# A graph network kernel's start and end: where the scale search, the last power, the ring writes and the last row sums stand

## What is computed

```python
# layer 0
h = max(layernorm(x), 0)
mask = adj > 0
e[b,j,k,:] = relu(h[b,j] @ W1a + (h[b,j] - h[b,k]) @ W1b + b1)   # H = 192
hm[b,j,:] = sum over k of e[b,j,k,:] * mask[b,j,k]
x = x + hm @ W2 + deg * b2                                        # deg = row sums of mask
# layer 1
h = max(layernorm(x), 0)
x = x + (adj @ h) @ W.T
```

## Time and profile before

| | us |
|---|---|
| runs, median (lowest to highest, 3 runs) | 842.24 (841.91 to 843.48) |
| the profiled execution, in all | 845.98 |
| its span, first to last instruction | 844.1 |
| PE busy in the span | 810.6 (96%) |
| DVE busy | 809.9 (96%) |
| ACT busy | 794.9 (94%) |
| POOL busy | 611.5 (72%) |
| mean granted clock of PE | 0.98 |

### The profile page before, as it was taken

The page is one execution under the profiler, slowest core; times in us unless marked ns, Lnnn a source line. Parts: engine busy times, 40 slices in busy tenths (PEclk is TensorE's granted clock), DMA queues, the critical chain, the costliest instruction groups (busy, mean ns, idle before and its releaser), DMA issues.

```text
span 844.1 us, 26648 instructions
## 1 busy us (share of the span) xinstructions
PE 810.6 (96%) x8242; PEld 715.0 (85%) x8243; DVE 809.9 (96%) x2894; ACT 794.9 (94%) x2246; POOL 611.5 (72%) x1174
## 2 busy tenths in 40 slices
PE   4879999999999999999999999999999999999996
PEld 2447888898889888988998899888988898889884
DVE  6969999999999999999999999999999999999993
ACT  4969999999999999999999999999999999999992
POOL 1966777777777777777777777777777777777762
PEclk8979999999999999999999999999999999999996
DMA  9800000000000000000000000000000000000000
GB/s 337 327 1 2 7 9 21 21 21 15 21 20 21 9 21 21 20 15 21 21 21 9 20 21 21 15 21 20 21 9 21 21 20 14 21 21 21 15 3 21
DMA packets 26705, 27.55 MB, mean 33 GB/s; under 512 B 3520, under 2 KB 24512, under 8 KB 25536
## 3 DMA queue, kind: packets, MB, share of 16 engines
q1 hardware_dynamic: 25488, 25.37, 8.9%
q10 hardware_dynamic: 1072, 0.43, 0.2%
HBM read 21.59 MB, written 4.19 MB: 31 GB/s over the span
## 4 chain that ended last, share of the span: by engine, by line
PE 90%; DVE 4%; issue 2%; ACT 2%; DMA 1%; SPq 0%; ACTq 0%; DVEq 0%
PE ring L414 48%; PE ring L442 8%; PE prep L471 5%; PE post L514 4%; PE post L501 3%; PE post L508 3%; PE post L502 3%; PE prep L479 3%; PE prep L482 2%; PE prep L477 2%; DVE acc L826 2%; PE post L506 2%; DMA x_all<-x_nbf_dram 1%; PE prep L473 1%; DVE onehot_space L812 1%
## 5 line engine op out<-in xcount | busy, mean ns | idle before, releaser
L826 DVE SCALAR_TENSOR_TENSOR acc<-ring,acc 128x384 f32<-128x384 f32 x896 | 488.6, 545 | 0.6
L572 ACT COPY ring<-P 128x384 f32<-128x384 f32 x1024 | 466.6, 509 | 19.3 <-DVE acc L826 11.4
L414 PE MATMUL ring<-PQ,onehot_space 128*128 128x192 f16 x4096 | 417.0, 247 | 4.5 <-ACT ring L572 2.2
L414 PEld LDWEIGHTS ring<-PQ,onehot_space 128*128 128x128 f16 x4096 | 328.0, 99 | 39.4 <-issue 13.5
L922 POOL TENSOR_SCALAR start<-P,spare 128x192 f32<-128x192 f32 x128 | 128.4, 1003 | 134.8 <-ACT P L622 133.8
L946 POOL TENSOR_TENSOR row_space<-row_space 128x192 f32<-128x192 f32 x256 | 153.4, 599 | 25.3 <-ACT row_space L610 8.2
L812 DVE TENSOR_SCALAR onehot_space<-mask_all 128x512 f16<-128x512 f16 x512 | 158.1, 311 | 0.0
L442 PE MATMUL ring<-PQ,owner 128*128 128x384 f16 (+1 forms) x512 | 93.9, 306 | 0.0
L414 PE MATMUL ring<-PQ,onehot_row 128*128 128x192 f16 x768 | 84.3, 246 | 0.5 <-DVE onehot_row L874 0.3
L610 ACT ACTIVATE row_space<-ring 128x576 f32<-128x576 f32 x128 | 83.3, 651 | 0.7 <-PE ring L414 0.7
L826 DVE SCALAR_TENSOR_TENSOR acc<-ring,start 128x384 f32<-128x384 f32 x128 | 71.1, 556 | 5.3 <-PE ring L414 1.3
(11 more groups left out here) (138 smaller groups left out, 1431.9 us busy)
## 6 DMA issues: line engine op xcount, KB each, us to landing
onehot_space<-adj_kbj_dram SPq DMA_DIRECT2D x8, 1024.0 KB, 17.3
adj_again<-adj_kbj_dram SPq DMA_DIRECT2D x128, 64.0 KB, 2.0
x_all<-x_nbf_dram SPq DMA_DIRECT2D x8, 512.0 KB, 19.0
out_dram<-x_all SPq DMA_DIRECT2D x32, 128.0 KB, 1.9
consts<-consts_dram SPq DMA_DIRECT2D x1, 192.0 KB, 2.4
scratch<-w1a_dram ACTq DMA_DIRECT2D x2, 48.0 KB, 4.2
scratch<-w1b_dram ACTq DMA_DIRECT2D x2, 48.0 KB, 6.7
scratch<-b_dram ACTq DMA_DIRECT2D x1, 96.0 KB, 10.1
```

What stands on the lines that cost most here:

```text
L414: last = nc.tensor.matmul(to, hot(s), parts[:, part, H:2 * H], start=False, stop=(part == 1), skip_group_check=True)
L572: return nc.scalar.copy(slots[to][:, bank_], src.unsqueeze(1).broadcast_to([N, PER_BANK, H]))
L826: return nc.vector.scalar_tensor_tensor(sums, slots[to][:, bank_], 0.0, start[:, :, :] if first else sums, ALU.max, ALU.subtract if first ...
```

## The change

- **PE**: codes(1) to codes(3) run whole, then L398; codes(4), then L402; the loop has parts 5 and 6 only. In every step the wait for the row sums stands between L501 and L502 instead of ahead of L501. After the codes, ring banks 0 to 3 are written before the tables, with a `ring_ready` of their own.
- **DVE**: `largest()` stands behind mask 2, `largest_of_rows()` behind mask 4, `scale()` behind mask 5, `second_parts()` behind mask 6. The four one-hots of chunk 0 come ahead of the wait for the last copies, two of chunk 1 ahead of the tables. In step 128 DVE adds the last graph's rows, which POOL did.
- **ACT**: L654 stands behind codes(4) and the two lead steps; parts 1 to 3 are a loop, part 4 is written out, 5 to 7 a loop. The steps begin when `any_loops` and the first `ring_ready` are there; chunk 2 of graph 0 waits for the second. In the tail both h2 of a pair are made together, those of the last pair behind the sums' copy of step 132.
- **POOL**: norm1(3) stands right behind norm1(2), ahead of the `spare` chain; `load_any` comes after the first `start`.
- **SP**: the last four graphs are stored two by two.

Unchanged lines are cut except next to a change, and indentation is reduced by eight.

```diff
--- before.py
+++ after.py
@@ -369,16 +369,17 @@
             adj(b + BODY + 1)
-    sp.wait_ge(y_ready, B // 2)
-    sp.dma_start(out[:, B - STORE:B, :], x_all[:, B - STORE:B, :]).then_inc(stored, 16)
-    sp.wait_ge(stored, 16 * B // STORE)
+    for done in range(B - STORE + 2, B + 1, 2):
+        sp.wait_ge(y_ready, done // 2)
+        sp.dma_start(out[:, done - 2:done, :], x_all[:, done - 2:done, :]).then_inc(stored, 16)
+    sp.wait_ge(stored, 16 * (B // STORE - 1 + STORE // 2))
...
 def _(pe):
-    def codes(g, quads=range(QUADS)):
+    def codes(g):
         pe.wait_ge(mask_ready, g + 1)
-        for q in quads:
+        for q in range(QUADS):
             quad = g * QUADS + q
@@ -392,15 +393,17 @@
     codes(0)
-    codes(1, range(QUADS // 2))
+    codes(1)
+    codes(2)
+    codes(3)
...
                      stop=True).then_inc(largest_seen, 1)
-    codes(1, range(QUADS // 2, QUADS))
+    codes(EARLY)
     pe.wait_ge(largest_ready, 2)
     nc.tensor.matmul(post[:, N:N + 1], ones_row[:, :], to_scale[0:1, 1:2], start=True, stop=True).then_inc(largest_seen, 1)
-    with pe.Fori(2, LATE) as g:
+    with pe.Fori(EARLY + 1, LATE) as g:
         codes(g)
@@ -494,11 +497,11 @@
                     pe.wait_ge(summed, b * REGULAR)
-                    pe.wait_ge(hm_row_ready, b)
                     if not main:
...
                         nc.tensor.matmul(head_ps, acc_space[:, (u - 1) // 2 % 2, s, heads[(u - 1) % 2]], ident, start=(s == 0), stop=False, is_transpose=True)
+                    pe.wait_ge(hm_row_ready, b)
                     last = nc.tensor.matmul(head_ps, row_heads[(u - 1) % 2], ownerT[:, (u - 1) % QUAD, :], start=False, stop=True)
@@ -526,18 +529,17 @@
 
-    pe.wait_ge(rows_counted, 1)
-    nc.tensor.matmul(tables[:, 0, :], ones[:, :], rows, start=True, stop=True)
-    nc.tensor.matmul(tables[:, 1, :], rows, ones[:, :], start=True, stop=True).then_inc(rows_summed, 1)
...
     pe.wait_ge(code_kj_ready, B // QUAD)
-    pe.wait_ge(code_jk_ready, B // QUAD)
-    write_ring(range(QUADS))
+    write_ring(range(QUADS)).then_inc(ring_ready, 1)
+
+    pe.wait_ge(rows_counted, 1)
+    nc.tensor.matmul(tables[:, 0, :], ones[:, :], rows, start=True, stop=True)
+    nc.tensor.matmul(tables[:, 1, :], rows, ones[:, :], start=True, stop=True).then_inc(rows_summed, 1)
@@ -571,6 +573,17 @@
 
+    def second_norm(b, u, t):
+
+        wait_apart(act, norm2_ready, pairs(b, u, t, -5 if u % 2 else -6))
+        if exists(b - 9):
+            act.wait_ge(transposed, transposes(b - 2 if u % 2 else b - 3))
+        k = (u - 5) // 2 % 2
+        for g in range(2) if not exists(b - 1) else ((u - 5) % 2,):
+            of = b - 5 - (u - 5) % 2 + g
+            nc.scalar.activation(h2[:, k, 2 * g, :], x_all[:, of, :], ACT.Relu, bias=shift2[:, k, g:g + 1],
+                                 scale=rstd2[:, k, g:g + 1]).then_inc(h2_ready, 1)
@@ -578,6 +591,8 @@
                     act.wait_ge(p_ready, b + 1)
+                if i == 2 and isinstance(b, int) and b == 0:
+                    act.wait_ge(ring_ready, 2)
                 if i == 2 and exists(b - 1):
@@ -597,6 +612,8 @@
                 nc.scalar.copy(sums_T[:, parts, :], sums_T_ps[:, parts, :]).then_inc(even_T_ready, 1)
+            if i == 0 and isinstance(b, int) and b == B + 4:
+                second_norm(b - 1, u - 1, t)
             if i == 0 and u % 2 and exists(b - 2):
@@ -620,14 +637,8 @@
                 nc.scalar.copy(P[:, (u + 1) % 2, :], pq_ps[:, 0:H]).then_inc(p_ready, 1)
-            if i == 4 and exists(b - 5):
-
-                wait_apart(act, norm2_ready, pairs(b, u, t, -5 if u % 2 else -6))
-                if exists(b - 9):
-                    act.wait_ge(transposed, transposes(b - 2 if u % 2 else b - 3))
-                k, g = (u - 5) // 2 % 2, (u - 5) % 2
-                nc.scalar.activation(h2[:, k, 2 * g, :], x_all[:, b - 5, :], ACT.Relu, bias=shift2[:, k, g:g + 1],
-                                     scale=rstd2[:, k, g:g + 1]).then_inc(h2_ready, 1)
+            if i == 4 and exists(b - 5) and (u % 2 or exists(b - 1)) and not (isinstance(b, int) and b == B + 3):
+                second_norm(b, u, t)
             if i == 4 and exists(b + 3):
@@ -648,19 +659,18 @@
     codes(0)
-    codes(1)
-    codes(2)
+    with nc.scalar.Fori(1, EARLY) as g:
+        codes(g)
+    codes(EARLY)
+    act.wait_ge(norm1_ready, 1)
+    lead(step, hi=-1)
     act.wait_ge(scale_ready, 1)
...
                          scale=to_scale[:, 2:3]).then_inc(first_parts_ready, 1)
-    codes(3)
-    act.wait_ge(norm1_ready, 1)
-    lead(step, hi=-1)
-    with nc.scalar.Fori(EARLY, PARTS) as g:
+    with nc.scalar.Fori(EARLY + 1, PARTS) as g:
         codes(g)
...
     some = load_any(nc.scalar)
-    act.wait_ge(tables_ready, 1)
     act.wait_ge(ring_ready, 1)
@@ -752,30 +762,43 @@
 
+    def hot(b, u, i, s):
+
+        return nc.vector.tensor_scalar(onehot[:, hot_of(u), i, s, :, :], code_kj[:, bass.ds(b, QUAD), :],
+                                       2.0 * (SLOTS * i + s) + 1.0, None, ALU.is_equal)
+
+    def first_hot():
+
+        for s in range(SLOTS):
+            last = hot(0, 0, 0, s)
+        last.then_inc(onehot_ready, 1)
...
     norm1_stats(1)
+    mask(2)
     largest()
-    mask(2)
-    largest_of_rows()
     moments(0)
     norm1_stats(2)
-    scale()
     mask(3)
     norm1_stats(3)
+    mask(4)
+    largest_of_rows()
     moments(1)
-    mask(4)
-    second_parts()
     mask(5)
+    scale()
     norm1_stats(4)
     mask(6)
+    second_parts()
     norm1_stats(5)
...
     moments(3)
+    dve.wait_ge(code_kj_ready, 1)
+    first_hot()
@@ -787,9 +810,8 @@
 
-    dve.wait_ge(p_ready, 1)
-    second_part(0, 0)
-
+    hot(0, 0, 1, 0)
+    hot(0, 0, 1, 1)
     dve.wait_ge(rows_summed, 1)
@@ -800,23 +822,21 @@
     nc.vector.tensor_scalar(loops[0:1, 1, :], fits[0:1, :], -float(LOOPED), float(LOOPED), ALU.mult, ALU.add)
+    nc.vector.tensor_copy(row_count[:, :], owned)
+    dve.wait_ge(p_ready, 1)
+    second_part(0, 0)
     dve.wait_ge(owned_sums, 1)
     nc.vector.tensor_scalar(loops[0:1, 0, :], tables[0:1, 3, :], float(LOOPED), None, ALU.mult)
-    nc.vector.tensor_copy(row_count[:, :], owned)
     chain(nc.vector.tensor_tensor(first_row[:, :], tables[:, 2, :], owned, ALU.subtract))
...
 
-    def hot(b, u, i, s):
-
-        return nc.vector.tensor_scalar(onehot[:, hot_of(u), i, s, :, :], code_kj[:, bass.ds(b, QUAD), :],
-                                       2.0 * (SLOTS * i + s) + 1.0, None, ALU.is_equal)
...
         i = u % QUAD
-        if exists(b - i + QUAD):
-            last = hot(b - i + QUAD, u - i + QUAD, i, s)
+        of = b - i + QUAD
+        if exists(of) and not (isinstance(of, int) and of == 0 and i == 1 and s < 2):
+            last = hot(of, u - i + QUAD, i, s)
             if s == SLOTS - 1:
@@ -829,6 +849,13 @@
         at = bass.ds(b + 1, 1)
+        if not main and b == B:
+
+            dve.wait_ge(relu_row_ready, B)
+            sums = relu_rows[(u - 1) % 2][:, 0, :]
+            nc.vector.tensor_tensor(sums, sums, relu_rows[(u - 1) % 2][:, 1, :], ALU.add).then_inc(half_row_ready, 1)
+            dve.wait_ge(half_row_ready, B)
+            nc.vector.tensor_tensor(sums, sums, relu_rows[(u - 1) % 2][:, 2, :], ALU.add).then_inc(hm_row_ready, 1)
         for i in range(CHUNKS):
@@ -908,9 +935,6 @@
 
-    for s in range(SLOTS):
-        last = hot(0, 0, 0, s)
-    last.then_inc(onehot_ready, 1)
     lead(step)
@@ -937,7 +961,7 @@
             nc.gpsimd.tensor_tensor(x_all[:, of, :], x_all[:, of, :], bias[:, :, :], ALU.add).then_inc(xb_ready, 1)
-        if exists(b - 1):
+        if exists(b - 1) and exists(b):
@@ -1009,6 +1033,7 @@
     norm1(2)
+    norm1(GROUPS - 1)
@@ -1019,12 +1044,10 @@
     pool.wait_ge(spare_step, 3)
-    some = load_any(nc.gpsimd)
-    pool.wait_ge(tables_ready, 1)
     pool.wait_ge(p_ready, 1)
...
     lead(step, lo=-1)
-    norm1(GROUPS - 1)
+    some = load_any(nc.gpsimd)
     graphs(nc.gpsimd, step, some)
```

## The result

The changed kernel takes 844.63 us (median of 20 runs, lowest 843.18), the kernel before on the same chip 842.7 (20 runs): ratio 1.0026, 95% interval 1.0019 to 1.0034. In a second comparison the ratio was 1.0029 (1.0017 to 1.0042). One of the 20 runs took 1020.49 at a mean granted clock of 0.75, and the ratio leaves it out. The prediction was 838.8 with 841.4 as its upper end: wrong in sign and outside its range.

The account below looks back on a forecast made before the run. PE and DVE were taken to bound the middle, its length unchanged. Front 2.3, end 1.0 and last store 0.1 summed to 3.4, taken from the median 842.24: 838.8 us, range 836.8 to 841.4.

Parts of the forecast that it names:

- the sentence on the middle: Middle steps, PE busy 99.69 and DVE 99.53 of 100 us: the change gains only by an earlier start and shorter end.
- Slower: PE's clock: Rival, first steps: over 10 us more at PE's lower clock make the change slower; with 12 us 844.8; chance 0.05.
- The opening: 2.3 predicted: Up to graph 0's first accumulation: POOL's chain ends last, so L826 comes at 54.6 instead of 56.92, 2.3 us gained.
- Quad 8 at 18.85: ACT's copies in the opening: quad 8 is copied at 18.85 instead of 20.51, 1.66 us earlier.
- I take 0.7 of the waits as covered: ACT's loop entry: 0.7 of 2.7 us of operations and waits is hidden, bounds 0 and 1.3; L593 comes at 44.5.
- DVE's stalls of 0.45 and 1.4: DVE in the opening: it stands 0.45 us ahead of L709 and 1.4 ahead of scale(), with no loss to ACT.
- L1003 at 34.8: POOL's chain in the opening: L1003 moves from 32.61 to 34.8, and norm1(2)'s power follows at 39.75.
- After the copies: Tables and one-hots before graph 0: tables 0.7 us later, one-hots 1.6 less, net 0.9 earlier; owner's product at 53.7.
- 56.92: Time of the first L826 in the profiled execution of the kernel before; the front gain was taken from it.
- The copies don't move: Rival, opening: mask 3 wait takes 1.1 and loop entry covers nothing, so copies end 0.6 us earlier; 839.6, chance 0.14.
- POOL late: Rival, POOL's opening chain: both powers take 6.33, 1.7 us more, giving 840.5, or 841.1 with a late scale search; chance 0.16.
- The end: 1.0 + 0.1 predicted: Kernel's end: DVE's adds and L501 ahead of the wait gain 1.0 us, bounds 0.5 and 1.3; the halved store 0.1.

Follow-up runs that it names:

- front_pad1: The changed kernel with one more DVE memset, as after_pad1, but with the end of the kernel before: 842.76 us, ratio 0.9997 to the kernel before.
- after_pad1: The changed kernel with one more memset of an unused column among DVE's first instructions: 840.83 us, ratio 0.9978 to the kernel before.
- copy_pad: The changed kernel with one unused one-column copy more on DVE, ahead of its wait for the row sums: 843.70 us, ratio 0.9980 to the kernel before.
- tail_only: The kernel before with all edits at the end alone, the moved wait for the row sums included: 841.14 us, ratio 0.9984 to the kernel before.
- after_again: The changed kernel unchanged, run again for a second trace: 845.36 us, ratio 1.0029 to the kernel before.

## Why the prediction was wrong

**The step that failed** is the sentence on the middle: "nothing in the change shortens that work, so it pays only by letting the middle start earlier and by shortening what follows". I took its length as given and never asked whether it could grow. It grew: steps 8 to 127 take 714.18 to 717.78, mean 715.7, in the nine traces without the stall and 718.52 to 721.13, mean 719.4, in the seven with it: 3.8 us, more than the 3.4 of my sum. In the time, one memset more on DVE moves the changed kernel from 1.0029 to 0.9978, 4.3 us. What the runs showed in place of the fixed length is that it depends on where in DVE's stream, counted modulo 128, the steps' first accumulations fall. No rival had it. "Slower: PE's clock" had the sign and another mechanism, and the trace speaks against it: the granted clock is 1.00 all through steps 8 to 127.

**The opening: 2.3 predicted, 0.8 measured.** Step 8 starts at a mean of 104.8 in the five traces with before's opening, and at 104.0 in the nine with the new one and norm1(3) ahead. In the time, the opening alone (front_pad1, 0.9997) isn't told from nothing. Step by step:

- Quad 8 at 18.85: it came at 18.91. The wait ahead of quad 12 was taken as 0.75 and measured 0.38 (in the other traces of the new opening up to 1.23). Right. The hole of 2.76 is gone as said; what stands ahead of 18.91 is 1.58 of waiting for part 2's mask, which can't come sooner.
- "I take 0.7 of the waits as covered" at the loop entry: wrong. From 23.30 to 45.10 lie 20 quads, 19.0 of copying, and 2.8 of other time, where before it was 2.7. Nothing was covered, my lower bound, and h1T came at 45.10 instead of 44.5.
- DVE's stalls of 0.45 and 1.4: 0.56 and 1.50. L1003 at 34.8, the power at 39.75, the next to 45.5, `start` done at 54.6: 34.81, 39.75, 45.48 and 54.67. The whole chain through three engines was right to 0.1.
- After the copies: PE's first product with `owner` was to come at 53.7 and came at 54.52. 0.6 of that are the later copies. In the five traces with the full clock at the ring writes and the power ahead it came at 52.08 to 52.91, in the four others at 54.52 to 55.48. My sum took PE's times from a trace at the lower level and had no term for the other. DVE was to be ready at 54.4 and was at 55.28: it began the one-hots later, and the last two, beside POOL's `start`, took 0.49 each where I had taken 0.27.
- Of this, 56.92 was itself a late value: the other traces of the old opening have the first accumulation at 56.04 to 56.93, those of the new one at 55.11 to 56.06.

**The rivals.** "The copies don't move" described the opening of the profiled execution in part (loop entry not covered, but the wait ahead of quad 12 was short). POOL's `start` ends last, as I had said, in seven of the nine traces with the power ahead, but at 55.1 to 56.0 instead of 54.6. That is "POOL late" by its effect and not by its mechanism: the two powers took 5.44 and 5.46 to 5.78, not 6.33, and the first of them began at 39.75 to 40.82 instead of 39.75. My reading that a power stood beside thirteen one-hots was wrong too: in the earlier trace rows they end at 55.64, and the power starts at 55.45. In copy_pad everything of DVE and PE is early, the owner's product at 52.69, and DVE stands for POOL.

```profile
55.72 0.56 DVE L848 SCALAR_TENSOR_TENSOR acc<-ring,start 128x384 f32<-128x384 f32 x1 [2.59 <-POOL start L948]
```

With PE at the lower clock both chains end within 1 us of each other; with the full clock POOL's ends 2.3 to 2.6 later, and where its power was moved back DVE's one-hots beside POOL's work came last (54.54 and 55.51). Speeding up one chain alone kept the gain small each time.

**The end: 1.0 + 0.1 predicted.** The row sums are 0.83 earlier, against the 1.0 that I took; for the halved store no gain shows, against 0.1 (from the start of DVE's last residual to the end 3.19 to 3.67 with it and 3.19 to 3.63 without); tail_only as a whole gives 1.3 (0.2 to 2.5). That DVE's statistics come later costs nothing, as said, though POOL starts its norm at 830.45 and not at 829.4: PE next waits for a residual of DVE (at 834.21, 0.38). Right.

**The sum** as the runs have it: 0.8 and 1.3 gained, 3.8 lost, 1.7 slower. The ratio of 1.0026 makes 2.2 (1.6 to 2.9) of 842.7. Without the stall the same change gives 0.9978, 1.9 faster, a little over half of what I had forecast.

## What to carry to other kernels

An engine that is 99% busy over hundreds of repeated steps can lose more to where its instruction stream happens to be cut than an edit of its ends can win. When a change moves the count of instructions ahead of a long loop or an unrolled body, compare the length of the *untouched* steps in both traces first; if a few are long at fixed numbers, add one idle instruction to that engine and time again before judging the change. And never read a difference of 0.3% from one trace of each: here the two first traces had the wrong sign.

## What the runs showed of the hardware

**DVE's stream has a cut every 128 records.** The stalls of 0.13 to 0.47 stand where a step's first accumulation, which waits for other engines, has a number 63 above a multiple of 128; one number later (after_pad1, copy_pad and before) it isn't held up. Near such a place the trace has one packet of 8 KB of instructions, in the window 232.4 to 232.9 of after and in 230.4 to 232 of after_pad1:

```profile
q14 instruction: 1, 0.01, 3.8%
```

```profile
q14 instruction: 1, 0.01, 1.8%
```

That holds for all 16 traces: of the 481 DVE records from number 319 on whose number is 63 above a multiple of 128, 480 have a packet of 8 KB of this queue that starts within 1 us of them; of records at other places in the 128 typically one in ten has. So the period of 128 is that in which DVE's instructions are loaded. The packet is there with the stall and without it, and at the 28 stalls it starts 0.66 to 0.95 *behind* the start of the held-up accumulation, so this packet is not what the accumulation waited for. 8 KB for 128 instructions would be 64 bytes each, which is what the Trainium skill (Perfetto Trace Analysis, The 4-stage abstract model) gives an instruction. The Trainium skill (Runtime: NRT & Kernel Launch, Terms) says that an engine's instruction memory is refilled in blocks of 16 KiB; for this queue the packets of this trace are half of that. What holds the accumulation up at the cut, and why only on that side of it, no run here shows.

**An operation of DVE and one of POOL that overlap can get longer, either of them.** `from_first` took 0.64 beside POOL's add and 0.24 without; three row one-hots 0.89 and 0.40; POOL's power 6.56 with two of DVE's masks beside it (27.35 and 32.81) and 5.44 at 39.75, where DVE makes statistics and moments up to 44.41. The Trainium skill (SBUF — State Buffer, Who interferes with whom) says that a DVE instruction in a two-port mode and a GpSimd instruction contend for a shared pair of ports, and that whichever issues first has it for the whole instruction. The lengths in these rows agree with that; in which mode the operations ran they don't show. Such an overlap makes a stall of 0.3 into a long step.

**When the clock falls at the end differs from execution to execution.** Windows of 833 to 835 in two executions of the changed kernel, the first profiled and then after_again, the granted clock third from the end:

```profile
833.00:835.00 2.00, 1.17 (x6) 0.82 (x6) 0.74 (x5) 0.27 (x2) 1.20 (x4) 1.00 0.00 0
```

```profile
833.00:835.00 2.00, 1.55 (x7) 1.28 (x6) 0.89 (x5) 0.40 (x2) 0.66 (x3) 0.50 0.00 0
```

The first stayed at 2.4 GHz until 14.3 behind the start of step 127, the second until 9.0 behind it. From that start to the end of the span they take 18.44 and 21.27. That is 2.8 us between executions of one kernel, more than all edits at the end together. In the other traces too the end is the longer the earlier the clock fell. With the new end, the nine others take 20.75 where the clock fell 9.3 behind, 19.71 and 19.84 where it fell 11.4 and 11.5 behind, and 18.47 to 18.94 from 13.2 to 14.5. With the old end it is 22.26 at 8.9, the first trace of before, and 20.03 to 20.63 from 13.7 to 15.1. So at a like clock the new end is 1.0 to 1.8 shorter, and the 844.1 from which the prediction started had an early fall in it.
